# VectorE's order inside a Householder reflection, wider idle matmuls in the last quarter, and Euler tiles on three PSUM banks, on one Trainium2 core

## What is computed

```
# layer 0: 8 Euler steps of a graph ODE on h = relu(layernorm(x))
h = h @ fc_in_w.T + fc_in_b
repeat 8:  h += (0.5*sigmoid(alpha)*(adj @ h - h) + h @ (w*clip(d)@w.T) - h + h0) / 8
x += h
# layer 1: spectral filter with the eigenvectors of a symmetric 512 x 512 matrix
deg = A.sum(0) + A.sum(1) - diag(A);  L_norm = d^-1/2 (diag(deg) - A) d^-1/2
_, U = eigh(L_norm)
x += U @ (relu((U.T @ h) @ W1 + b1) @ W2 + b2)
# layers 2 and 3: a graph convolution with batch norms; two graph convolutions and windowed LSTMs
```

## Time and profile before

| | us |
|---|---|
| three runs | 4682.31, 4701.35, 4705.41 (median 4701.35) |
| the profiled execution's own time | 4695.59 |
| its span, first to last instruction | 4693.8 |
| TensorE busy in the span | 3295.6 (70%) |
| VectorE busy | 3012.1 (64%) |
| ScalarE, GpSimd busy | 1019.7, 787.2 |
| first L1490 (reflection 1) to the last (510) | 95.2 to 2336.0 |
| mean granted TensorE clock | 0.746 |

### The profile page before, as it was taken

One profiled execution on the slowest core, in us unless ns is written; L12 is line 12 of the kernel. 1 busy time (PEld: TensorE's weight loads), 2 busy tenths in 40 slices (PEclk: granted clock), 3 DMA queues, 4 the chain that ended last, 5 costly groups with the idle time before them and its releaser, 6 DMA issues.

```text
span 4693.8 us, 71717 instructions
## 1 busy us (share of the span) xinstructions
PE 3295.6 (70%) x21732; PEld 2284.9 (49%) x21732; DVE 3012.1 (64%) x18157; ACT 1019.7 (22%) x3735; POOL 787.2 (17%) x3360
## 2 busy tenths in 40 slices
PE   2999998999999899999900101000357586799998
PEld 1777776777776677888700000000234432344433
DVE  6647887888788878777778889999531224002323
ACT  0212222222222322222200000000013212315542
POOL 1111222222222322222222221111000000000000
PEclk7758997899799788555555555555688897789998
DMA  2000000000000000000000000000000000000000
GB/s 90 2 1 2 2 2 2 2 2 2 2 2 2 2 2 2 1 1 1 1 0 0 0 0 0 0 0 0 0 0 0 18 0 0 0 0 0 0 0 36
DMA packets 3102, 21.13 MB, mean 5 GB/s; under 512 B 432, under 2 KB 560, under 8 KB 1072
## 3 DMA queue, kind: packets, MB, share of 16 engines
q1 hardware_dynamic: 2736, 16.85, 0.9%
HBM read 12.66 MB, written 4.19 MB: 4 GB/s over the span
## 4 chain that ended last, share of the span: by engine, by line
PE 46%; DVE 38%; issue 6%; ACT 5%; POOL 4%; DMA 0%; DVEq 0%; POOLq 0%; ACTq 0%; SPq 0%
PE ps L934 6%; DVE H L1764 5%; PE ps L608 4%; PE ps L649 4%; DVE jq L1366 3%; PE ps L941 2%; POOL step L995 2%; PE ps L653 2%; PE ps L641 2%; DVE H L1366 2%; DVE XYEG L1504 2%; ACT sz L1202 2%; PE ps L659 2%; PE ps L602 2%; POOL C L996 2%
## 5 line engine op out<-in xcount | busy, mean ns | idle before, releaser
L649 PE MATMUL ps<-C 128*32 128x131 f32 (+39 forms) x10200 | 415.0, 298 | 7.7 <-DVE C L1583 3.9
L995 POOL TENSOR_SCALAR step<-XYEG,PQ 128x8 f32<-128x8 f32 (+3 forms) x510 | 161.3, 316 | 1219.7 <-DVE PQ L1520 1219.7
L608 PE MATMUL ps<-C,LT 128*128 128x256 f32 x1024 | 338.2, 444 | 0.0
L608 PE MATMUL ps<-WK,LT 128*128 128x256 f32 x1024 | 338.1, 444 | 0.0
L1202 ACT ACTIVATE sz<-C,PQ 128x4 f32<-128x4 f32 (+3 forms) x510 | 151.6, 297 | 791.9 <-POOL C L996 791.9
L658 PEld LDWEIGHTS ps<-dots,ones 128*128 128x128 f32 x1020 | 207.4, 237 | 213.3 <-DVE dots L1366 178.7
L649 PEld LDWEIGHTS ps<-C 128*32 128x32 f32 x10200 | 276.1, 123 | 55.9 <-DVE C L1583 13.0
L1186 ACT ACTIVATE tsc<-tsc 128x1 f32<-128x1 f32 x510 | 103.4, 203 | 878.6 <-DVE tsc L1490 878.6
L934 PE MATMUL ps<-C,V 128*128 128x512 f32 (+1 forms) x504 | 287.5, 727 | 8.5 <-issue 7.5
L1366 DVE CUSTOM_DVE_ANT_0 jq<-SO,ps,C 128x10 f32<-128x10 f32 (+14 forms) x1199 | 220.1, 228 | 97.8 <-PE ps L669 50.1
L658 PE MATMUL ps<-dots,ones 128*128 128x2 f32 x1020 | 213.2, 279 | 77.9 <-DVE dots L1366 57.8
(11 more groups left out here) (479 smaller groups left out, 7735.8 us busy)
## 6 DMA issues: line engine op xcount, KB each, us to landing
out_x<-X SPq DMA_DIRECT2D x4, 1024.0 KB, 3.9
X<-in_x SPq DMA_DIRECT2D x2, 1280.0 KB, 20.6
X<-in_x SPq DMA_DIRECT2D x1, 1536.0 KB, 16.9
eye<-in_eye SPq DMA_DIRECT2D x1, 1026.0 KB, 9.5
WK<-in_adj SPq DMA_DIRECT2D x1, 1024.0 KB, 4.9
adjT<-in_adjT SPq DMA_DIRECT2D x1, 1024.0 KB, 7.0
WK<-in_below SPq DMA_DIRECT2D x1, 1024.0 KB, 11.0
V<-in_wih SPq DMA_DIRECT2D x1, 1024.0 KB, 4.9
```

The lines of the kernel that those rows point to most:

```text
L608: m = mm(some, LT[:, mb, j * P:(j + 1) * P], state(k + 1)[:, 2 * half:2 * half + 2, mb, :], start=False, stop=(part == last), skip_group_c ...
L649: m = mm(ps[q * QUAD:(q + 1) * QUAD, 0, 0:c + n], SI[:, b, 0, 2 * j:2 * j + 1].broadcast_to([P, QUAD]), AS[:, b, q, k * QUAD:P + n], start ...
L995: step(g_.tensor_scalar(step2[:, k:KB, :], this[:, :, 2:4], PQ[:, r % 2, 1:2], None, ALU.mult))
```

## The change

Four parts.

1. VectorE's order in a reflection. With two or more active blocks the reciprocal of the root stands ahead of the reduction, the fused step on it (`c1`) ahead of the dot products, and `sgx` behind them. In every quarter `next4` now stands ahead of `uz`, and `cc` ahead of `tz`. With one or two blocks `uy` stands ahead of the product for `ns2, sn`. `sgx` reads the PSUM bank that L659 writes; so TensorE now waits for `beta_ready` before L659 in quarters 0 to 2.
2. `IDLE` is a number per quarter: 384 columns in quarter 3. (The others are used only after the last piece, which now is in quarter 3.)
3. Tiles rotate over three banks (4, 5, 6) instead of four; the units `w` use bank 7 and are spread, at most one piece in a reflection, first in its pause, among tiles that no longer wait for them. Only a tile's last step with k = 0 waits for `w`.
4. `ROOM` is (2, 2) in quarter 2 too; `PANEL_ROOM` gives one piece less at the panel changes of quarters 0 and 1.

By the planner's tables the first tile piece now stands at reflection 16, units `w` run from 17 to 93, the last tile is copied out at reflection 400, and idle matmuls start at 402. The group changes lie at 114 to 131, 207 to 223 and 300 to 316.

```diff
-IDLE = 256
-ROOM = ((2, 2), (2, 2), (2, 1), (1, 1))
-PANEL_ROOM = ((1, 2, 4), (1, 2, 3), (1, 1, 1), (1, 1, 1))
+IDLE = (256, 256, 256, 384)
+BANKS = 3
+ROOM = ((2, 2), (2, 2), (2, 2), (1, 1))
+PANEL_ROOM = ((1, 2, 3), (1, 2, 2), (1, 1, 1), (1, 1, 1))
...
+            while i in self.taken or self.early(i, after) or one and (self.slots[i][0][1] > 0 or i > 0 and self.slots[i - 1][0] == self.slots[i][0]):
+                i += 1
+            self.taken.add(i)
...
+    start, w = i, ("out", 0)
     for u in range(EULER + 1):
-        p.unit(("w", u), [[last]] * (2 * KB if u > 0 else KB))
-        last = ("w", u)
-    first = 1
+        i, _ = p.unit(("w", u), [[w]] * (2 * KB if u > 0 else KB), i, one=True)
+        w = ("w", u)
+    i, first, out = start, 1, ("out", 0)
     for t in range(4 * TILES):
-        free = [("tile", t - 4)] if t >= 4 else [last]
+        free = [("tile", t - BANKS)] if t >= BANKS else [out]
...
             def pause(r, h):
-                if len(pieces) == 0 and r > EULER_END:
+                idle = IDLE[min(r // P, KB - 1)]
+                if len(pieces) == 0 and r > EULER_END and idle > 0:
                     pe.wait_ge(S["eu_sb"], 4 * TILES)
-                    keep_clock(IDLE)
+                    keep_clock(idle)
...
                 mm(ps[:, 3, 0:2], ones[:], dots[:], start=True, stop=True).then_inc(S["dots_ps"], 1)
+                if k < KB - 1:
+                    pe.wait_ge(S["beta_ready"], r)
                 mm(ps[:, 1, 1:2], spread(XYEG[:, r % 2], k, 2), XYEG[:, r % 2, k, 3:4], start=True, stop=True).then_inc(S["pivot_ps"], 1)
...
                 m_sg = ch.mark(ts_(sg, x1, 0.0, -0.5, ALU.is_lt, ALU.add))
+                if nb > 1:
+                    dve.wait_ge(S["root_ready"], r)
+                    m_rc = ch.mark(v.reciprocal(rc, root))
+                    ch.need(m_prod)
+                    v.tensor_reduce(y, terms, AX.X, ALU.add).then_inc(S["y_ready"], 1)
+                    ch.need(m_rc)
+                    m_c1 = ch.mark(stt(c1, rc, nsq, root, ALU.mult, ALU.add))
+                    dve.wait_ge(S["y_ready"], r)
+                    go(ttr(jk[:, 0, k:KB], x, y, dots[:, 0:1]))
+                    ttr(jk[:, 1, k:KB], e, y, dots[:, 1:2]).then_inc(S["dots_in"], 1)
+                    ch.need(m_c1)
+                    m_sgx = ch.mark(tt(sgx, x1, sg, ALU.mult))
+                    ch.need(m_sgx)
...
                 stt(pair, tsc[:, 3:5], c1, tsc[:, 0:2], ALU.mult, ALU.subtract).then_inc(S["beta_ready"], 1)
...
+                if nb < 3:
+                    dve.wait_ge(S["dots_ps"], r)
+                    m_uy = ch.mark(stt(uy, mu, y1, xy, ALU.mult, ALU.subtract))
...
+                ch.need(m_uy)
+                m_cc = ch.mark(tt(cc, uy, sn, ALU.mult))
                 dve.wait_ge(S["pivot_ps"], r)
                 m_tz = ch.mark(stt(tz, mu, g1, y1, ALU.mult, ALU.subtract))
-                ch.need(m_tz)
-                m_uz = ch.mark(stt(uz, tz, mu, uy, ALU.mult, ALU.subtract))
                 ch.need(m_cc)
                 m = stt(next4, four(xb), cc, four(yb), ALU.mult, ALU.add)
...
+                ch.need(m_tz)
+                m_uz = ch.mark(stt(uz, tz, mu, uy, ALU.mult, ALU.subtract))
```

More of the change, by code:

```diff
@@ L127, in __init__ @@
         self.tensor, self.scalar, self.pool = {}, {r: [] for r in range(REFLECTIONS + 4)}, {r: [] for r in range(REFLECTIONS + 4)}
-        self.next, self.seen = 0, {}
+        self.taken, self.seen = set(), {}
     def at(self, key, r):
@@ L135, in at, with unit, early @@
         return r
-    def unit(self, key, parts):
+    def unit(self, key, parts, start=0, one=False):
+        i = start
         for part, needs in enumerate(parts):
             after = max([0] + [self.seen[n] for n in needs])
-            while self.slots[self.next][0] < (after, 1) or after > 0 and self.slots[self.next][0][0] == after and self.slots[self.next][0][1] > 1:
-                self.next += 1
-            at, root = self.slots[self.next]
+            while i in self.taken or self.early(i, after) or one and (self.slots[i][0][1] > 0 or i > 0 and self.slots[i - 1][0] == self.slots[i][0]):
+                i += 1
+            self.taken.add(i)
+            at, root = self.slots[i]
             self.tensor.setdefault(at, []).append(key + (part,))
-            self.next += 1
-        return self.at(key, root)
+            i += 1
+        return i, self.at(key, root)
+    def early(self, i, after):
+        r, h = self.slots[i][0]
+        return (r, h) < (after, 1) or (h > 1 and r == after > 0)
 def plan_gaps():
@@ L168, in plan_gaps @@
                     first = p.at(("input", 8 * g + h), first) + 1
[L169 removed]
+            i, _ = p.unit(("tile", t), [free + [("input", 8 * g + 2 * j + 1)]] * 2, i)
         elif k == EULER:
[L171 removed]
+            i, _ = p.unit(("tile", t), [free + [("tile", t - 1 - j)]] * 2, i)
         else:
[L173 to L174 removed]
+            i, r = p.unit(("tile", t), [free] * 2 + [[("tile", t - j - 4 + mb)] for mb in range(KB) for _ in range(2)]
+                          + ([[w]] * 2 if k == 0 else []), i)
             if k == 0:
@@ L1502, in reflect @@
                 m_sg = ch.mark(ts_(sg, x1, 0.0, -0.5, ALU.is_lt, ALU.add))
[L1503 to L1510, removed]
-                    both = XYEG[:, r % 2, k, :].rearrange("p (t s) -> p s t", s=2)[:, 0, :]
-                    m = tt(dots[:], both, y.broadcast_to([P, 2]), ALU.mult)
-                else:
-                    go(ttr(jk[:, 0, k:KB], x, y, dots[:, 0:1]))
-                    m = ttr(jk[:, 1, k:KB], e, y, dots[:, 1:2])
@@ L1516, in reflect @@
-                m.then_inc(S["dots_in"], 1)
-                ch.need(m_rc)
-                m_c1 = ch.mark(stt(c1, rc, nsq, root, ALU.mult, ALU.add))
-                ch.need(m_c1)
+                if nb > 1:
[11 more added lines that the diff above has]
+                    ch.need(m_sgx)
+                else:
+                    both = XYEG[:, r % 2, k, :].rearrange("p (t s) -> p s t", s=2)[:, 0, :]
+                    ch.need(m_prod)
+                    v.tensor_reduce(y, terms, AX.X, ALU.add).then_inc(S["y_ready"], 1)
+                    dve.wait_ge(S["root_ready"], r)
+                    m_rc = ch.mark(v.reciprocal(rc, root))
+                    ch.need(m_sg)
+                    go(tt(sgx, x1, sg, ALU.mult))
+                    dve.wait_ge(S["y_ready"], r)
+                    tt(dots[:], both, y.broadcast_to([P, 2]), ALU.mult).then_inc(S["dots_in"], 1)
+                    ch.need(m_rc)
+                    m_c1 = ch.mark(stt(c1, rc, nsq, root, ALU.mult, ALU.add))
+                    ch.need(m_c1)
```

32 lines of the change are left out of this document (16 added, 16 removed).

## The result

The changed kernel is faster. The median of 4 runs is 4550.38 us (4529.63 to 4556.20) against 4691.83 of 4 runs of the kernel before on the same chip (4680.09 to 4705.41): ratio 0.969 [0.9645, 0.9734]. The forecast was 4577 in 4530 to 4650. The profiled execution took 4556.2 us, its span is 4554.4, 139.4 shorter than before.

The account below looks back on a forecast made before the run. The bound was taken as a loop across engines at full clock, and TensorE itself at half clock in quarter 3. Terms -65 - 84 + 9 + 10 - 6 + 2 + 10 = -124 gave 4577 us, range 4530 to 4650.

Parts of the forecast that it names:

- Early stretch: Reflections 16 to 47: tiles among units `w` raise the clock, -65 us, with 16 to 24 left at the old pace.
- Quarter 3: Idle matmuls of 384 columns from 402 raise the clock and keep it up: -84 us, 2.97 us a reflection.
- Half cold and half warm: Reflections 402 to 415, taken as partly at each clock level, at no net gain.
- Rival 1: Quarter 3 stays at 1.2 GHz, since TensorE is already saturated there: 4763 us, slower; 10%.
- Rival 2: The clock in quarter 3 rises and falls back again and again: 4670 us; 6%.
- Rival 3: The early stretch stays cold to reflection 48: 4642 us; 8%.
- Rival 4: The earlier `next4` counts, with L649 in quarter 0 following `x_ready`: about 4537 us; 15%.
- The wait: TensorE's wait for beta before L659: +0.12 us in about 75 full reflections of quarter 0, +9 us; hidden in quarters 1 and 2.
- The order: VectorE's new order, with the reciprocal pushing the reduction by about 0.12 us in quarter 2: +10 us in all.
- together beta moves: Beta's shift under the new order: +0.06 us in quarter 2, +0.03 in quarter 1, 0.03 earlier in quarter 0, hidden under L649.
- The one-row matmuls: One-row matmuls of `w` in full pauses up to reflection 93: +2 us.
- Group change: The first group change moves back to 114 to 131, so eight more of its reflections are of quarter 0: +10 us.

Follow-up runs that it names:

- b_plan: The kernel before with the new plan alone (VectorE's old order, no wait for beta, idle matmuls of 256 columns): 4608.8 us, ratio 0.982.
- a_old: The changed kernel with VectorE's old order and without TensorE's wait for beta: 4528.74 us, ratio 0.9643.
- a_256: The changed kernel with idle matmuls of 256 columns instead of 384 in quarter 3: 4620.45 us, ratio 0.9842.
- a_old_wait: The changed kernel with VectorE's old order but TensorE's wait for beta kept in quarters 0 to 2: 4562.36 us, one run.
- a_norow: The changed kernel without the one-row matmul in units `w` after the first: 4533.31 us, one run.
- a_fill: The changed kernel with idle matmuls in every empty pause after the last unit `w`, group changes included: 4520.63 us, ratio 0.9637.
- a_q0old: The changed kernel with the old order up to beta and no wait for beta in quarter 0 only: 4536.08 us, ratio 0.9663.

## Why the prediction was right, and where its terms were off

**The forecast's mechanism holds.** Two stretches went from 1.2 to 2.4 GHz, for -65 - 84 forecast and -75.4 and (quarter 3 as a whole, 500.1 to 416.1) -84.0 measured. The measured median is 27 us below the forecast. Of that, 15 come from the profiled execution, which fell by 139.4 and not by 124. The rest is scatter: the profiled execution after was 5.8 slower than its median, the one before 5.8 faster. The small terms together were forecast at +25 and measured +20, but not one by one, and 8.6 of the 20 lie in reflections 1 to 15 with equal code; that the sum fits is partly luck.

**Early stretch, -65, measured -75.4.** The plan alone gives -79 (b_plan). I had left reflections 16 to 24 at the old pace, at a cost of 25 us; they took 47.2 us, 5 above the new pace. Against that, reflections 25 to 47 took 4.43 in the median (panel changes apart) and not the 4.2 I gave as a sign, in part for the one-row matmuls.

**Quarter 3, -84, measured -84.0, by two errors that cancel.** The five panels gave 82.9 and not 71, since a reflection takes 2.81 and not 2.97; of that 0.11 is the order (a_old: 2.92), and the remaining 0.05 my estimate's. That 384 columns fit and add nothing held: the warm reflection 417 takes 2.77 with 256 (a_256) and with 384 columns, and 2.91 with 512. The last 15 gave 14.4 for 13. Against it, reflections 402 to 415 were counted at no net gain and cost 12.5, as none of them was warm: at 1.2 GHz the wide matmuls lengthen a reflection to 4.7 us, and the clock came only with the panel change. "Half cold and half warm" is the step that was wrong here.

**Rival 1** fell. Its reading, that more columns can't lift a full engine, is refuted by the two kernels that differ in the width alone: 256 columns 307.5 us at 0.57, 384 columns 237.75 at 1.00. TensorE was busy 99% of the time with 256 columns at 1.2 GHz and 99.9% with 384 at 2.4. The Trainium skill (TensorE: Matmul & The Clock Gate, Part 1) sets the gate by how busy the engine has been; these rows agree only if "busy" there isn't the profile's busy share. **Rival 2** shows only in the panel 400 to 415 and in a_256. **Rival 3** fell (0.87). **Rival 4** fell in quarter 0, where `next4` ends 0.44 before L664, and holds in quarter 3, where I had written that nobody could use it; it isn't enough to shorten the whole (a_old).

**The wait, +0.12, measured +0.16** in full reflections of quarter 0 (a_old_wait, one run), of which the order takes 0.06 back: +0.10 net, by luck near the forecast, which had called the order hidden there. In quarters 1 and 2 it is hidden, as forecast.

**The order, +10, measured about nothing in quarter 2 and a gain elsewhere, with a price that I hadn't seen.** The root does push the reduction (0.41 to 0.50 after the norm in the medians of quarter 2, a_old against after), by 0.10 for the 0.12 forecast. But the steps before `pair` save more than I counted: norm to `pair` goes from 1.115 to 1.128 in quarter 2, +0.01 for the +0.06 of the step "together beta moves", from 1.215 to 1.179 in quarter 1, where +0.03 was expected, and from 1.317 to 1.254 in quarter 0, for -0.03. The median reflection changes by -0.01 (3.485 to 3.478) and by -0.05 (3.817 to 3.764). That step is the one mis-sized. Quarter 3, counted at 0, gave -0.11 in 95 reflections. In no term at all stood the stall of the last section: 10.2 us, as much as the whole term.

**The one-row matmuls, +2, measured more** (a_norow, one execution): +9.6 in reflections 48 to 111, of which 4.4 are the row's own and the rest may be the clock's, and +6.8 in 16 to 47. The step that was off is the size: each row in a full first pause costs its reflection a quarter of a microsecond, and 20 of the 46 reflections from 48 to 93 now carry one.

**One piece less in a panel change, -6**: at 63, 79 and 111, where the granted clock is 0.87 in both kernels, the panel change is 0.2 to 0.4 us shorter, for the 0.43 counted; the new order is in that too.

**Group change, +10**, measured +12.2 in 112 to 127 and -9.1 in 128 to 143, so +3.1: the change moved, and its cost grew less than forecast. a_fill shows what it is, a stretch at 1.2 GHz. **Rest of quarters 1 and 2, 0**: -1.1, within the spread. Reflections 1 to 15 have equal code and cost +8.6 by the clock's phase; nothing forecast that.

## What to carry to other kernels

The profile's busy share of TensorE doesn't say which clock it will get (99% at either level here): try idle matmuls at two widths and read granted clock and reflection time together. A warm stretch is best not broken: filling the pauses at the group changes gave 30 us, while bringing the clock back in quarter 3 first cost 12.5. Before counting an earlier result as useless, ask in each stage who starts at its end once the clock is high: what waited for TensorE at 1.2 GHz in quarter 3 waited for VectorE at 2.4. And read a reordering's total beside its parts: here each part that got shorter was real, and the kernel without the new order was no slower.

## What the runs showed of the hardware that was not expected

GpSimd's add of 128x512 holds one of VectorE's operations back. In the kernel before, the column of SO (L1545) starts ahead of the add, and the product behind it runs beside the add at 0.22:

```profile
730.68 0.25 DVE L1545 SCALAR_TENSOR_TENSOR SO<-C,tsc,sz 128x4 f32<-128x4 f32 x1
...
730.86 1.27 POOL L1004 TENSOR_TENSOR X<-X,C 128x512 f32<-128x512 f32 x1
...
731.07 0.22 DVE L1366 CUSTOM_DVE_ANT_0 jq<-SO,ps,C 128x6 f32<-128x6 f32 x1
```

In the changed kernel `x_ready` and with it GpSimd's copies come earlier, and the add starts first. The copies come earlier by `next4`'s place: a_q0old, with the old head in quarter 0, has the stall as often.

```profile
642.58 1.28 POOL L1021 TENSOR_TENSOR X<-X,C 128x512 f32<-128x512 f32 x1
...
642.60 1.28 DVE L1575 SCALAR_TENSOR_TENSOR SO<-C,tsc,sz 128x4 f32<-128x4 f32 x1
...
644.02 0.24 DVE L1383 CUSTOM_DVE_ANT_0 jq<-SO,ps,C 128x28 f32<-128x28 f32 x1
```

The operation with all its inputs in SBUF takes 1.14 to 1.28 us instead of 0.21 to 0.25, in 11 of the 16 adds (11.2 us in all), in 14 of 16 where quarter 3 is wide from 384 (14.1 us), and in none before or with the old order. In the five adds of the changed kernel ahead of which it started it took 0.21 to 0.22. A stall lengthens its reflection by about as much: 197 takes 5.00 us in the changed kernel and 3.98 in a_old, 200 takes 4.82 and 3.81. The product that reads PSUM isn't held. The Trainium skill, GPSIMD Engine Reference, in its table of section 1, says that GpSimd shares its SBUF interface with VectorE and contends with VectorE's instructions of two SBUF inputs; these rows agree and give the price. The hold isn't new with the order: in the kernel before, L1512, a product of two SBUF inputs, took 0.43 instead of 0.14 once, beside such an add. What is new is that the column of SO falls behind the start of the add, which neither the diff nor the order of instructions on one engine shows.
